# Tiles of a cross-attention and mixture-of-experts kernel turned as f32r, two rounding copies moved from ScalarE to GpSimd

## What is computed

```python
D, H, KVH, DK = 512, 16, 2, 32          # attention; x and ctx are (8, 512, 512) f32
def _L0_xattn_ref(query, key, value, mask, wq, wk, wv, wo):
    Q = (query @ wq).reshape(B, L, H, DK).transpose(0, 2, 1, 3)
    K = (key @ wk).reshape(B, L, KVH, DK).transpose(0, 2, 1, 3)
    V = (value @ wv).reshape(B, L, KVH, DK).transpose(0, 2, 1, 3)
    ...
    Q = _rope(Q, pos)
    K = _rope(K, pos)
    scores = jnp.einsum('bhqd,bhkd->bhqk', Q, K) / math.sqrt(DK)
    scores = jnp.where(mask == 0, -1000000000.0, scores)
    attn = jax.nn.softmax(scores, axis=-1)
    ...
    return out @ wo

def _L0_ffn_ref(x, Wr, Wg, Wu, Wd, Sg, Su, Sd, expert_bias):   # 8 experts, 2 per token, F = 256; FS = 512
    logits = xf @ Wr + expert_bias
    top_v, top_i = jax.lax.top_k(logits, K)
    ...
    h = jax.nn.silu(gate) * up
    eo = jnp.einsum('tef,efd->ted', h, Wd)
    out = jnp.einsum('te,ted->td', rw, eo)
    out = out + jax.nn.silu(xf @ Sg) * (xf @ Su) @ Sd
...
x = x + _L0_xattn_ref(_layernorm(x, axis=-1), ctx_1024, ctx_1024, mask, wq, wk, wv, wo)
x = x + _L0_ffn_ref(_layernorm(x, axis=-1), Wr, Wg, Wu, Wd, Sg, Su, Sd, expert_bias)
```

## Time and profile before

| | |
|---|---|
| median of 3 runs | 1426.14 us (1424.04 to 1426.2) |
| the profiled execution: first to last instruction | 1422.9 us |
| granted TensorE clock, mean | 0.994 of full |
| start | 0 to 43 us |
| attention, first batch, six middle ones, last and end | 43 to 129, 129 to 666, 666 to 769 us |
| dense stage, routed stage | 769 to 1055, 1055 to 1423 us |
| busy: TensorE, VectorE, ScalarE, GpSimd | 97%, 67%, 59%, 41% of the span |

### The profile page before, as it was taken

How to read it: one execution, slowest core, us unless ns; L and a number is a source line. 1 busy time by engine, 2 the same in 40 slices (tenths; PEclk the granted TensorE clock), 3 DMA queues, 4 the chain that set the end, 5 groups by cost and what they waited for, 6 DMA issues and landing times.

```text
span 1422.9 us, 28293 instructions
## 1 busy us (share of the span) xinstructions
PE 1373.1 (97%) x8110; PEld 1067.2 (75%) x8110; DVE 960.4 (67%) x2655; ACT 844.9 (59%) x1951; POOL 581.4 (41%) x724
## 2 busy tenths in 40 slices
PE   6898999999999999999898999999999999999997
PEld 4675777877777777777576777777777888888885
DVE  6888888888888888988777666666653334333342
ACT  2788979889798897988983222222213434444342
POOL 4443523435244343342253432333334555555553
PEclk9899999999999999999999999999999999999999
DMA  5545464564645646445465222222257779785542
GB/s 203 152 145 146 135 190 139 152 185 137 188 136 149 187 131 190 142 140 157 114 202 203 85 87 90 82 75 84 73 140 205 201 178 260 204 197 103 111 76 37
DMA packets 146070, 206.62 MB, mean 145 GB/s; under 512 B 35456, under 2 KB 73088, under 8 KB 145923
## 3 DMA queue, kind: packets, MB, share of 16 engines
q1 hardware_dynamic: 124562, 166.91, 38.1%
q0 software_dynamic: 17952, 33.64, 12.3%
q10 hardware_dynamic: 3408, 4.26, 0.9%
HBM read 105.49 MB, written 69.35 MB: 123 GB/s over the span
## 4 chain that ended last, share of the span: by engine, by line
PE 82%; DVE 6%; ACT 4%; issue 3%; DMA 2%; SPq 1%; POOL 1%; DVEq 0%; POOLq 0%; ACTq 0%
PE psum L693 13%; PE psum L1494 13%; PE psum L1496 12%; PE psum L1495 12%; PE psum L808 7%; PE psum L787 7%; PE psum L738 3%; PE psum L739 3%; PE psum L740 3%; ACT a_probs L591 2%; PE psum L1561 2%; PE psum L708 2%; DVE a_probs L955 1%; ACT a_probsT L597 1%; PE psum L1590 1%
## 5 line engine op out<-in xcount | busy, mean ns | idle before, releaser
L591 ACT ACTIVATE a_probs<-a_probs,a_low 128x512 f32<-128x512 f32 x512 | 366.6, 716 | 83.7 <-DVE a_low L955 82.2
L955 DVE CUSTOM_DVE_ANT_0 a_probs<-psum,a_bias 128x512 f32<-128x512 f32 x512 | 345.4, 685 | 76.5 <-PE psum L787 73.2
L693 PE MATMUL psum<-a_ident,a_probs 128*128 128x128 f32 x2048 | 311.0, 274 | 7.8 <-ACT a_probsT L597 5.9
L693 PEld LDWEIGHTS psum<-a_ident,a_probs 128*128 128x128 f32 x2048 | 245.3, 141 | 77.0 <-issue 25.6
L787 PE MATMUL psum<-a_kT,a_q_stack 128*128 128x512 f32 x512 | 247.2, 484 | 10.1 <-DVE a_low L955 5.4
L597 ACT ACTIVATE a_probsT<-psum 128x512 f32<-128x512 f32 x328 | 190.7, 582 | 10.0 <-PE psum L693 10.0
L1363 POOL DMA_INDIRECT out<-b_y,b_pairs_sb x71 | 112.6, 1586 | 148.7 <-DMA out<-b_y,b_pairs_sb 85.9
L1795 DVE SCALAR_TENSOR_TENSOR b_v_hidden<-b_v_hidden,psum 128x256 f32<-128x256 f32 x71 | 29.9, 421 | 165.9 <-ACT b_v_hidden L1459 165.9
L961 DVE COPY a_probsT<-psum 128x512 f32<-128x512 f32 x184 | 126.0, 685 | 6.1 <-PE psum L693 4.2
L1494 PE MATMUL psum<-b_w,b_vT_hi 128*128 x284 | 117.4, 413 | 0.1
L808 PE MATMUL psum<-a_probsT,a_v 128*32 128x512 f32 x1024 | 116.7, 595 | 0.0
(11 more groups left out here) (218 smaller groups left out, 3054.3 us busy)
## 6 DMA issues: line engine op xcount, KB each, us to landing
b_w<-w_halves SPq DMA_DIRECT2D x16, 1536.0 KB
a_q_stack<-a_qT_hi SPq DMA_DIRECT2D x254, 64.0 KB, 2.0
a_q_stack<-a_qT_lo SPq DMA_DIRECT2D x253, 64.0 KB, 2.0
w_halves<-a_w_hi SPq DMA_DIRECT2D x96, 128.0 KB, 2.0
w_halves<-a_w_lo SPq DMA_DIRECT2D x96, 128.0 KB, 1.9
a_xT_in<-in_x_turned SPq DMA_DIRECT2D x32, 256.0 KB, 2.9
a_ctx_in<-in_ctx SPq DMA_DIRECT2D x32, 256.0 KB, 3.0
a_x_in<-in_x SPq DMA_DIRECT2D x32, 256.0 KB, 3.2
```

The costliest lines, as they stand in the source:

```text
L591: nc.scalar.activation(probs[:, h % 2, t], probs[:, h % 2, t], ACT.Exp, bias=low[:, h % H, t:t + 1], scale=-1.0, accum_out=total[:, h // G ...
L693: last = nc.tensor.transpose(out[:, P * i:P * (i + 1)], src(i), identity[:])
L955: nc.vector.tensor_tensor_reduce(probs[:, h % 2, t], psum[:, t % 2], bias[:, t], 1.0, HUGE, ALU.add, ALU.min, low[:, h % H, t:t + 1]).then ...
```

## The change

All transposes that were f32 are asked for as f32r: the sources (probabilities, q, normalised rows, gathered rows, hidden tile) are read through a second name of the same memory with type f32r (`bits`), the output in PSUM is named f32r, and the identity is `ident_r`. Nothing is rounded for it, and no instruction is added. `ident` and `ident_r` change places in memory, since the stages after attention now need the latter.

In attention, ScalarE's copies `turned_x` (but for those of the start) and `output_high` (but for the third group of the last batch and the one in the end) are gone; GpSimd makes them at the places at which it had the subtractions, right ahead of these.

```diff
-        def four(out, src, identity):
+        def four(out, src):
             for i in range(4):
-                last = nc.tensor.transpose(out[:, P * i:P * (i + 1)], src(i), identity[:])
+                last = nc.tensor.transpose(out[:, P * i:P * (i + 1)].bitcast(F32R), src(i), ident_r[:])
             return last
...
-            four(in_ring(part, b, "qT", i), lambda t: q[:, batch, t, P * g:P * (g + 1)], ident).then_inc(s["qT_filled"], 1)
+            four(in_ring(part, b, "qT", i), lambda t: q_bits[:, batch, t, P * g:P * (g + 1)]).then_inc(s["qT_filled"], 1)
...
-            four(out, lambda c: probs[:, h % 2, t, P * c:P * (c + 1)], ident).then_inc(s["t_filled"], 1)
+            four(out, lambda c: probs_bits[:, h % 2, t, P * c:P * (c + 1)]).then_inc(s["t_filled"], 1)
...
-                last = nc.tensor.transpose(psum[:, XT + n % 2, P * c:P * (c + 1)], xn[:, n % XN_SLOTS, P * c:P * (c + 1)], ident[:])
+                last = nc.tensor.transpose(psum[:, XT + n % 2, P * c:P * (c + 1)].bitcast(F32R), xn_bits[:, n % XN_SLOTS, P * c:P * (c + 1)], ident_r[:])
...
-                last = nc.tensor.transpose(psum[:, XT + n % 2, P * c:P * (c + 1)], rows[:, n % X_SLOTS, P * c:P * (c + 1)], ident[:])
+                last = nc.tensor.transpose(psum[:, XT + n % 2, P * c:P * (c + 1)].bitcast(F32R), rows_bits[:, n % X_SLOTS, P * c:P * (c + 1)], ident_r[:])
...
-                mm = nc.tensor.transpose(psum[:, HT + n % 2, P * i:P * (i + 1)], v_hidden[:, n % 2, i:F:FC], ident[:])
+                mm = nc.tensor.transpose(psum[:, HT + n % 2, P * i:P * (i + 1)].bitcast(F32R), v_hidden_bits[:, n % 2, i:F:FC], ident_r[:])
...
-        def x_low(b, t):
+        def turned_x(b, t):
+            pool.wait_ge(xT_loaded[t % 2], b * 32 + (48 + 16 * (t // 2)))
+            alone(pool, s["passed"])
+
+            wait_count(pool, s["q_filled"], upto(b, "q", t - 1))
+            alone(pool, s["passed"])
+            nc.gpsimd.tensor_copy(xT_hi[:], xT_in[:, t % 2]).then_inc(s["xT_rounded"], 1)
             pool.wait_ge(s["xT_rounded"], upto(b, "xT", t))
             nc.gpsimd.tensor_tensor(xT_lo[:], xT_in[:, t % 2], xT_hi[:].bitcast(F32), ALU.subtract).then_inc(s["xT_split"], 1)
...
-        def output_low(b, par, g):
+        def output_halves(b, par, g):
             at = att_slot(par, g)
+            pool.wait_ge(s["att_ready"], upto(b, "spread", g))
+            alone(pool, s["passed"])
+            nc.gpsimd.tensor_copy(attT_hi[:, at], att[:]).then_inc(s["att_rounded"], 1)
             pool.wait_ge(s["att_rounded"], upto(b, "spread", g))
...
-                if kind == "xT":
-                    turned_x(part, b, i)
...
-                if kind == "att_hi":
+                if kind == "att_hi" and part == "last" and i == HG - 2:
                     output_high(b, par, i)
```

21 lines of the change are left out of this document (15 added, 6 removed).

## The result

The changed kernel takes **1413.43 us** (median of 4 runs, 1410.48 to 1418.81), the kernel before 1426.02 on the same chip: a ratio of 0.9919, 95% interval 0.9899 to 0.9939. So it is faster, by 12.6 us, a fifth of the 61 us forecast, and 20 us above the range.

What follows compares the result with a forecast made beforehand. TensorE was taken as the bound, with 1 to 3 us of room per attention stretch. Savings of 48 us in attention, 4 in the dense and 9 in the routed stage made 61, giving about 1365 us, range 1331 to 1393.

Steps and rivals of the forecast that it cites:

- What bounds the kernel: Whole kernel: TensorE, busy 97% of the span, is the bound, with 1 to 3 us of room per attention stretch.
- 0.05 us goes from each transpose behind which the next weight load is a transpose's: All changed transposes: steps between starts fall from 0.11 us in f32 to 0.06 in f32r.
- the pair L715 is too short to show it: Rival, chance 0.05: loads of 128 columns take 0.11 us and set the pace, so nothing is gained; 1426 us.
- A group of four that is followed by a product saves 0.14: Groups of four transposes in attention and after: 0.14 us saved each, between 0.13 and 0.20.
- step 5 of the prediction: After attention: about 4 us (3 to 6) from 32 groups, and 9 us (5 to 20) from 71 routed visits.
- L1590 gains nothing and may lose 0.02: Routed stage's transpose pair reading every second column: both steps already sit at 0.11 us, so no gain, perhaps 0.02 lost.
- 19.3, 22.9, 20.9 and 19.5, 82.6 instead of 89.2 us: Middle attention batch, four successive stretches of sixteen slots and their sum: 6.6 us saved per batch, 39.6 for six.
- A: First of four sixteen-slot stretches of a middle attention batch: VectorE's 18.9 us plus 0.4 of coupling, 19.3 us.
- That rival, 1393: Rival, chance 0.14: coupling makes every attention stretch take 1.2 us more than its busiest engine; 33 us gained in all.
- It stands in line there: GpSimd's added copies in attention, 5 us per batch: hidden by idle time, at worst 0.2 us twice per batch.
- no new wait reaches them: GpSimd's queue in attention: q sum, k tile and weight pieces behind the added copies meet no new wait.
- The forecast is wrong if TensorE's clock drops in attention: Attention: a lower TensorE clock was named as a sign that the forecast fails, with no size given.

Runs made afterwards that it cites:

- half loads: The changed kernel, turning only 64 of the 128 columns of each source in attention, the rest left out: 1405.60 us, ratio 0.9861.
- half of the scores: The changed kernel, with VectorE's minimum and ScalarE's exponential over 256 of 512 columns, the rest left out: 1395.56 us, ratio 0.9798.

## Why the prediction was wrong

**What bounds the kernel**: right. TensorE was the bound, with 1 to 3 us of room per stretch. How little that is, I underrated.

**"0.05 us goes from each transpose behind which the next weight load is a transpose's"**: right for the first two of a group (0.060 and 0.065 instead of 0.109), wrong for the third, which gives 0.024. I took 0.06 from L728 (8 columns per load) and from a pair, L715. The one shows only what short loads allow, the other only a first step, with its load made ahead; behind the third full turning, and behind the fourth where there is a fifth, the step is 0.085. I had this as a rival ("the pair L715 is too short to show it") with 0.05, and with a price of no gain at all; the truth lies between, and half loads show the forecast's pace exactly.

**"A group of four that is followed by a product saves 0.14"**: it saves 0.07. Beside the third step the last one costs more: with 0.23 us for the scores, the 0.60 leave about 0.16 for it, where I took 0.13. That 0.13 rested on L708, whose steps of 0.11 I read as the pace of its loads, and the row can't show that: L708's operands are f32, each of its matmuls leaves two records, and f32 columns are slow by themselves. The L808 products, also f32, with 512 columns and loads of 32, start four together every 0.41 to 0.43 us, where an f32r product of 512 takes 0.23. The same number holds after attention (step 5 of the prediction): 71 visits at 0.07, less 0.02 for the pair, make 3.5 us, and the routed stage is 3.3 us shorter to the end instead of 9. Up to the routed stage it is 2.9 instead of 4, and part of that is chance: a block of the dense stage, with four groups, got 0.2 us shorter (37.3 to 37.1), under 2 in eight, while from the first dense product to the first visit kernels with the same f32r turnings take 291.0 to 294.0 us (before 293.8, changed 291.0). That L1590 gains nothing and may lose 0.02 was right in size, though not for the reason given, that both of its steps sit at 0.11: the pair and the start of the product behind it take 0.18 us (0.060 and 0.122), against 0.15 (0.113 and 0.036) before, and 0.01 of that comes back in the product.

**"19.3, 22.9, 20.9 and 19.5, 82.6 instead of 89.2 us"**: the shortest stretches are 19.6, 24.3, 22.3 and 20.9, 87.1, and the mean batch 88.6. The half loads split it. With my pace the shortest stretches are 19.4, 24.2, 21.4 and 20.5, 85.5. So per middle batch, of the 6.9 us that were to go (from the mean of 89.5):

- 2.9 us are **coupling** that I priced too low (85.5 against 82.6). In A, where I looked at VectorE's 18.9 us, I was right within 0.1. In B to D I let TensorE keep its own need plus 0.2 to 0.7, though VectorE had 20 to 22 us of work in B and C and ScalarE 19 in D. The unfilled stretches said 1.3 to 2.7 above the busiest engine, and I had set that aside for all but a rival. That rival, 1393, had the right mechanism and too small a size, for it still had my pace. Some 0.6 of the 2.9 are not waits for VectorE's minimum or the evacuation but what the half loads' shortest B and C still hold of `a_v` and the k piece (0.4 and 0.2).
- 1.6 us are the **pace** of the turnings (87.1 against 85.5).
- 1.5 us are what the shortest stretches don't show (88.6 against 87.1): GpSimd's k piece in slot 35, slots 20 and 24 (TensorE waits for `a_v` to leave its bank, longer in some batches than in others), and the spots of lower clock.
- 0.9 us were gained.

The half of the scores splits it from the other side: its shortest stretches are 18.2, 23.9, 21.8 and 20.0, 83.9, so that at the pace measured coupling costs 3.2 us (87.1 against 83.9) and 1.3 are left for the pace (83.9 against 82.6). Either way coupling is the larger part.

Six batches give 5.3 us. The first, forecast at 3.7 less, took 1.0 more (86.6 against 85.6), with A 2.0 us longer for the clock and B and the tail shorter; the last gave 0.7 instead of 4.5.

**"It stands in line there" (GpSimd)**: the x tiles, which I worked out, were on time: the cast starts at 344.82, the subtraction ends at 346.80, and TensorE takes the halves at 347.28; slot 29's 0.22 us are a wait for the minimum instead.

```profile
346.95 0.50 PE L800 MATMUL psum<-a_kT,a_q_stack 128*128 128x512 f32 x1 [0.39 <-DVE a_low L968]
```

But "no new wait reaches them" was wrong for the k piece, four longer pieces of work behind the added copy. The copies' relief for ScalarE was worth nothing by itself, as their move alone shows.

**"The forecast is wrong if TensorE's clock drops in attention"**: it does. I had named it and given it no price. The lower mean clock, 0.9865 for 0.993, is 2 x 0.0065 x 1411 = 18 us more at the lower level, worth 5 to 8 us at 0.26 (first batch) to 0.46 (a filled stretch) us for each; an estimate from these rows. The kernels that keep the clock up by f32 give as much away, so what naming it with a price would have changed stays small.

## What to carry to other kernels

Measure a pace on a run as long as the one it is wanted for, and in its form: the first steps of a row show what slack and preparation allow, not what can be sustained. When the bound engine is at 97% and two others stand at 90 to 95% of a stretch, with two buffers between them, count waits first: here 0.07 us less in each slot gave 3.65 us in 47 slots and gave 2.8 back in the others. And ask what an added piece of work stands in front of for the whole queue, four entries on, not only for its own consumer.

## What the runs showed of the hardware

- Turnings of 128x128 in f32 stand 0.109 us apart; asked for as f32r, 0.085 with loads of 128 columns from the third step on, 0.060 and 0.065 in the first two, and 0.060 with 64 columns. Products of 512 columns show the same ratio of the types: 0.41 to 0.43 us in f32 (four at a time, L808), 0.23 in f32r.
- Which type the turnings have bears on the granted clock. With f32 in attention it stays up in stretches where VectorE or ScalarE holds TensorE up (2.87 of 4 us busy at 120 us, clock 1.00); with f32r it falls in some of them to the lower level for 3.4 to 6.8 us at a time (2.90 of 4 us busy, 0.80), and at the start it returns later (at 54 us instead of 46.5) or, in five other kernels, falls again within 4 us of its return. A fifth f32r turning that fills the time doesn't hold it up. Why it doesn't, no run here tells, and with f32 in attention and f32r after it the mean clock of ten runs was 0.991, not 0.993.
